# The opening of the last mixture-of-experts stage: weights' rests, cleared rows and the first gathered tiles in another order

## The reference, cut to what matters

```
x: (4, 750, 192) after the stages before; 3000 tokens, D=192, F=768, E=8 experts
n      = layernorm(h)
logits = n @ Ws + bs                       # (tokens, 8)
probs  = softmax(logits);  route = argmax(probs);  prob_max = max(probs)
hid    = gelu(n @ W1[route] + b1[route])   # 192 -> 768
y      = hid @ W2[route] + b2[route]       # 768 -> 192
out    = h + prob_max * y                  # each token goes through one expert
```

## Time and profile before

| | us |
|---|---|
| median of 3 runs (1774.12 to 1779.3) | 1778.48 |
| profiled execution, device time | 1779.27 |
| its span in the trace | 1777.5 |
| last stage: first DVE instruction | 1547.54 |
| list of rows `take` written | 1598.11 |
| first product of the first gathered tile | 1614.67 |
| second gathered tile's turn of the loop begins | 1619.93 |

### The profile page before, as it was taken

One profiled execution on the slowest core, in us unless ns is written; L12 is line 12 of the kernel. 1 busy time (PEld: TensorE's weight loads), 2 busy tenths in 40 slices (PEclk: granted clock), 3 DMA queues, 4 the chain that ended last, 5 costly groups with the idle time before them and its releaser, 6 DMA issues. The chain is left out here.

```text
span 1777.5 us, 32284 instructions
## 1 busy us (share of the span) xinstructions
PE 1545.6 (87%) x10815; PEld 1432.0 (81%) x10816; DVE 1198.3 (67%) x2259; ACT 990.7 (56%) x1818; POOL 343.4 (19%) x507
## 2 busy tenths in 40 slices
PE   4873899945999999899999899899999999646997
PEld 4762899944899899898899899799999889526996
DVE  3878555547785786785787686687777587485553
ACT  6433222224777578577577678577668657262221
POOL 4130566650100110110010010010010000103443
PEclk6886899976998999999899999999999899757999
DMA  8203111145101101100110110110110100191121
GB/s 257 68 23 95 45 56 57 58 118 141 43 11 37 43 11 37 45 11 18 29 43 10 30 44 19 28 43 19 29 43 19 28 8 19 45 311 46 59 61 30
DMA packets 61940, 94.86 MB, mean 53 GB/s; under 512 B 15645, under 2 KB 46512, under 8 KB 61423
## 3 DMA queue, kind: packets, MB, share of 16 engines
q1 hardware_dynamic: 52606, 72.92, 13.9%
q0 software_dynamic: 9200, 20.21, 3.9%
HBM read 72.58 MB, written 21.06 MB: 53 GB/s over the span
## 5 line engine op out<-in xcount | busy, mean ns | idle before, releaser
L2690 DVE TENSOR_TENSOR a_Plo<-a_PT,a_Phi 125x756 fp32r<-125x756 f32 x288 | 281.9, 979 | 72.5 <-ACT a_PT L2415 71.5
L2415 ACT ACTIVATE a_Phi<-a_S 125x756 fp32r<-125x756 f32 x288 | 231.2, 803 | 152.0 <-PE a_O L2209 128.4
L2580 DVE TENSOR_REDUCE a_nmx<-a_M 125x1 f32<-125x752 f32 x248 | 232.7, 938 | 102.9 <-PE a_M L2084 101.9
L1904 POOL TENSOR_TENSOR a_qlo<-a_work,a_qhi 127x750 fp32r<-127x750 f32 x48 | 79.2, 1659 | 1012.6 <-PE a_S L2190 510.9
L2415 ACT ACTIVATE a_PT<-a_S 125x756 f32<-125x756 f32 x288 | 230.3, 800 | 0.0
L1129 PE MATMUL m_psG<-m_w,m_xT 128*128 x788 | 167.3, 351 | 5.1 <-issue 2.3
L2190 PE MATMUL a_S<-a_qhi,a_khi 128*125 128x378 f32 x576 | 153.5, 348 | 10.0 <-DVE a_nmx L2580 6.8
L2202 PE MATMUL a_O<-a_Phi,a_vhi 125*128 125x378 f32 x576 | 150.3, 342 | 1.4 <-issue 1.1
L2209 PE MATMUL a_O<-a_Plo,a_vhi 125*128 125x378 f32 x576 | 147.5, 337 | 0.4 <-DVE a_Plo L2690 0.2
L2190 PE MATMUL a_S<-a_qhi,a_klo 128*125 128x378 f32 x576 | 147.6, 338 | 0.0
L2190 PE MATMUL a_S<-a_qlo,a_khi 128*125 128x378 f32 x576 | 147.0, 336 | 0.0
(11 more groups left out here) (431 smaller groups left out, 3017.1 us busy)
## 6 DMA issues: line engine op xcount, KB each, us to landing
a_qhi<-a_rdens SPq DMA_DIRECT2D x48, 187.5 KB, 3.3
m_w<-in_m_w SPq DMA_DIRECT2D x16, 384.0 KB, 7.2
a_wkv<-a_w4k SPq DMA_DIRECT2D x8, 768.0 KB, 4.9
a_wq<-a_w4q SPq DMA_DIRECT2D x8, 768.0 KB, 6.3
a_wkv<-a_w4v SPq DMA_DIRECT2D x8, 768.0 KB, 5.9
m_w<-in_m_w SPq DMA_DIRECT2D x8, 576.0 KB
m_X<-m_xn SPq DMA_DIRECT2D x8, 504.0 KB
m_w<-in_m_w SPq DMA_DIRECT2D x16, 192.0 KB, 7.5
```

What stands on the lines that cost most here:

```text
L1904: pool.tensor_tensor(qlo[0:ONE, u % HG % QLO, :], work[0:ONE, u % HG, 0:L], qhi[0:ONE, u % HG, :].bitcast(F32), ALU.subtract).then_inc(sg[ ...
L2415: last = nc.scalar.activation(to[:, wd % 2, :].rearrange("p (a l) -> p a l", a=2), psS[wd % 2][0:P, :, 0:HP], ACT.Exp, scale=SCALE)
L2580: v.tensor_reduce(nmx[:, u % 2, c:c + 1], bank[0:P, :, 0:376], AX.XY, ALU.max, negate=True).then_inc(sg["max_ready"], 1)
L2690: v.tensor_tensor(Plo[:, wd % 2, :], PT[:, wd % 2, :], Phi[:, wd % 2, :].bitcast(F32), ALU.subtract).then_inc(sg["exp_rest"], 1)
```

## The change

- `BLO` becomes 65, next to `BHI`. The product with `xB` runs over rows 0 to 65, all of which are written by rest or bias. The eight memsets (L998) go, and with them SP's and PE's waits for them; PE waits for the ones in `xB` through a new semaphore `s_xo`. POOL's four clearing transfers follow `xB` at once.
- The subtraction of a rest is written as `scalar_tensor_tensor` (times 1.0, minus) in place of `tensor_tensor`.
- ACT rounds expert 3 behind the last logits, ahead of the exponentials; DVE makes its rest behind `msk`.
- Behind `take` DVE's queue reads: rests 4, 5, 6, `rest_of_tokens(0, 0)`, rest 7, `rest_of_tokens(0, 1)`, and only then the parts of the probability and `tileP`.
- PE turns the first two gathered tiles without waiting for weights; those waits stand behind the turns, ahead of the first product. That holds for the first mixture too, where nothing else changes.

```
-BHI, BLO = 64, 96
+BHI, BLO = 64, 65
...
-                sp.wait_ge(s_z, 3)
                 sp.wait_ge(s_wb, 18)
...
-                pool.memset(xB[64:128].bitcast(F32), 1.0)
-            if not cfg.gated:
-                for e in range(NE):
-                    last = pool.memset(w1[64:128, e, 3, :].bitcast(F32), 0.0)
-                last.then_inc(s_z, 1)
-                pool.wait_ge(s_z, 3)
+                pool.memset(xB[64:128].bitcast(F32), 1.0).then_inc(s_xo, 1)
+                pool.wait_ge(s_xo, 1)
...
-            pe.wait_ge(s_eid, 1)
-            pe.wait_ge(s_w, 16 * (NE + (0 if cfg.gated else 3)))
-            if not cfg.gated:
-                pe.wait_ge(s_wl, NE)
-                pe.wait_ge(s_z, 3)
             for j in range(2):
                 pe.wait_ge(s_in[j], 16)
                 if j:
                     pe.wait_ge(s_xc, 1)
                 to_columns(j)
             pe.wait_ge(s_xc, 2)
+            pe.wait_ge(s_eid, 1)
+            pe.wait_ge(s_w, 16 * (NE + (0 if cfg.gated else 3)))
+            if not cfg.gated:
+                pe.wait_ge(s_wl, NE)
+                pe.wait_ge(s_xo, 1)
...
             logits_out(NT // GROUP - 1)
+            if not cfg.gated:
+                round_weights(soon)
             act.wait_ge(s_ls, 1)
...
-                for e in range(soon, NE):
+                for e in range(soon + 1, NE):
                     round_weights(e)
...
-                v.tensor_tensor(w1[:, e, 1, :], w1[:, e, 1, :].bitcast(F32), w1[:, e, 0, :].bitcast(F32), ALU.subtract)
+                v.scalar_tensor_tensor(w1[:, e, 1, :], w1[:, e, 1, :].bitcast(F32), 1.0, w1[:, e, 0, :].bitcast(F32),
+                                       ALU.mult, ALU.subtract)
...
                 v.tensor_copy(msk[:], oh[:, 0]).then_inc(s_m, 1)
+                rest_of_weights(3)
...
-                for e in range(3, NE):
+                for e in range(4, NE):
+                    if e == NE - 1:
+                        rest_of_tokens(0, 0)
                     rest_of_weights(e)
+                rest_of_tokens(0, 1)
...
-            rest_of_tokens(0, 0)
-            rest_of_tokens(0, 1)
+            if cfg.gated:
+                for j in range(2):
+                    rest_of_tokens(0, j)
```

More of the change, by code:

```diff
@@ L918, in moe @@
         s_w1 = [] if cfg.gated else [sem(f"w1_{e}") for e in range(NE)]
-        s_wb, s_wh, s_wl = (None if cfg.gated else sem(k) for k in ("wb", "wh", "wl"))
+        s_wb, s_wh, s_wl, s_xo = (None if cfg.gated else sem(k) for k in ("wb", "wh", "wl", "xo"))
         s_xh = sem("xh")
@@ L1308, in rest_of_weights, with rest_of_tokens @@
                 dve.wait_ge(s_wh, e + 1)
-                v.tensor_tensor(w1[:, e, 1, :], w1[:, e, 1, :].bitcast(F32), w1[:, e, 0, :].bitcast(F32), ALU.subtract)
-                v.tensor_tensor(w1[0:64, e, 3, :], w1[0:64, e, 3, :].bitcast(F32), w1[0:64, e, 2, :].bitcast(F32),
-                                ALU.subtract).then_inc(s_wl, 1)
+                v.scalar_tensor_tensor(w1[:, e, 1, :], w1[:, e, 1, :].bitcast(F32), 1.0, w1[:, e, 0, :].bitcast(F32),
+                                       ALU.mult, ALU.subtract)
+                v.scalar_tensor_tensor(w1[0:64, e, 3, :], w1[0:64, e, 3, :].bitcast(F32), 1.0,
+                                       w1[0:64, e, 2, :].bitcast(F32), ALU.mult, ALU.subtract).then_inc(s_wl, 1)
+            def rest_of_tokens(i, j):
+                dve.wait_ge(s_xh, RING * i + (j + 1))
+                v.tensor_tensor(xT[:, j % 2, 1, :], psX[:, 0:SLOT], xT[:, j % 2, 0, :].bitcast(F32), ALU.subtract)
+                v.tensor_tensor(xT[64:128, j % 2, 2, :], psX[0:64, SLOT:2 * SLOT],
+                                xT[0:64, j % 2, 2, :].bitcast(F32), ALU.subtract).then_inc(s_xc, 1)
+                if not cfg.gated:
+                    v.tensor_copy(hres[:, j % RING, :], xg[:, j % RING, E:2 * E]).then_inc(s_hr, 1)
             def normalise(t):
@@ L1501, in _ @@
             v.sem_inc(s_y, 1)
-            def rest_of_tokens(i, j):
-                dve.wait_ge(s_xh, RING * i + (j + 1))
-                v.tensor_tensor(xT[:, j % 2, 1, :], psX[:, 0:SLOT], xT[:, j % 2, 0, :].bitcast(F32), ALU.subtract)
-                v.tensor_tensor(xT[64:128, j % 2, 2, :], psX[0:64, SLOT:2 * SLOT],
-                                xT[0:64, j % 2, 2, :].bitcast(F32), ALU.subtract).then_inc(s_xc, 1)
-                if not cfg.gated:
-                    v.tensor_copy(hres[:, j % RING, :], xg[:, j % RING, E:2 * E]).then_inc(s_hr, 1)
             def gated_hidden(i, j):
```

## The result

The changed kernel takes 1765.95 us (median of 8 executions), the kernel before in the same comparison 1777.53 (8 executions): ratio 0.9941, 95% interval 0.9923 to 0.9959. One of the eight had a granted clock of 0.563 where the others had 0.926 to 0.935 and took 2825.08 us; the ratio leaves it out, and the median of the other seven is 1765.15. A second comparison, with 12 and 17 executions, gave 1768.51 and 1776.13, ratio 0.9952 [0.9934, 0.9970]. The change gains 0.5 to 0.6%, some 9 us. The predicted 1770.5 against 1778.48 is a ratio of 0.9955.

What follows compares the result with a forecast made beforehand. DVE was taken to bound the stretch before the last stage's loop, working 13 us without a gap, and PE the loop behind its first turns. -2.4 + 0.3 - 6.4 + 0.5 = -8.0 us gave 1770.5 us; 8-in-10 range 1767 to 1774.5.

Steps and rivals of the forecast that it cites:

- front: Start of the last stage: without the memsets DVE's first six normalised tiles run faster, last logits 2.4 us earlier.
- expert 3's rounding ahead of the exponentials: On ACT behind the last logits copy: one rounding of 2.44 us delays the exponentials, costing 0.3 us.
- queue behind the list: DVE's new order behind the list of rows: the first product of a gathered tile comes 6.4 us earlier.
- PE's wait for `tileP`: Ahead of the probabilities' products: PE finishes the first products before `tileP` is ready, a new wait costing 0.5 us.
- PE's clock: Around the first products: the clock's rise may move by a microsecond or two either way, half counting: +-1; no chance given.
- turns of the loop: Loop over gathered tiles in the last stage: turns were said to last as long as before.
- The middle of the range: 2.4 us for the front, between 1.9 and 2.9, since which clock PE gets there could not be read.
- the hole of 1.74 us: DVE's wait for PE's counts, said to hold expert 3's rests of 1.74 us at no cost, 0.1 at most.
- The wait for the first gathered tile: On DVE behind rests 4, 5, 6: 0.96 us of new idle time until gathered tile 0's rest can start.
- The form: DVE's rests as `scalar_tensor_tensor` in place of `tensor_tensor`: no difference in time expected.
- Neither rival on it: Rests in the new form: slower by 0.78 us each, 1781.0, chance 0.04; or POOL freed for gathers, 1769.6, chance 0.12.
- The rule of the Trainium skill: For DVE's rests: the new form with two sources that aren't bf16 runs at half throughput, 0.78 us more each.

Runs made afterwards that it cites:

- x3: Changed kernel with expert 3 rounded behind the exponentials and its rests made behind the list again; one profiled execution took 1767.57 us.
- x8: Changed kernel with the probability's sum and quotient ahead of gathered tile 0's rest, PE's register load and expert 3's first rounding copy earlier; median 1766.96 us, ratio 0.9938.
- x1: Changed kernel with the eight memsets of the third weight rows and the waits for them put back; one profiled execution took 1779.79 us.
- x2: Changed kernel with the rests written as `tensor_tensor` again; one profiled execution took 1766.19 us.
- x7: Changed kernel with PE loading the first expert's register ahead of its waits for tile 1's rest and the weights; one profiled execution took 1765.36 us.
- x11: Changed kernel with thirty transposes of the identity added on PE in each of the two mixtures, run again; median 1758.02 us, ratio 0.9891.
- x12: Changed kernel with thirty transposes of the identity added on PE in the last mixture alone; median 1768.39 us, ratio 0.9952.
- x5: Changed kernel with DVE doing the probability's sum, quotient and parts first behind the list, ahead of the rests; one profiled execution took 1766.12 us.
- x10: Changed kernel with thirty transposes of the identity added on PE in each of the two mixtures, first run; one profiled execution took 1750.82 us.
- x6: Changed kernel with the probability's sum and quotient put into DVE's 0.98 us wait ahead of gathered tile 0's rest; one profiled execution took 1777.52 us.

## Why the prediction was right

The milestones give each term of the sum.

| term | predicted | measured | by |
|---|---|---|---|
| front | -2.4 (-1.9 to -2.9) | -2.2 | A -1.95 less the next row |
| expert 3's rounding ahead of the exponentials | +0.3 | +0.3 | x3 and x8: A 48.3 without, 48.6 with |
| queue behind the list | -6.4 | -6.27 | B 16.56 to 10.29 |
| PE's wait for `tileP` | +0.5 | +0.3 | PE's row at 1609.91 |
| PE's clock | 0 (+-1) | -0.7 | C -0.36 less the row above |
| turns of the loop | 0 | -0.3 | last 157.56 to 157.28, all of it in the second turn's own length (4.92 to 4.62) |
| sum | -8.0 | -8.86 | A, B, C and last |

**The front.** That the memsets slowed DVE's normalised tiles was right (x1), and so was the size. The tiles take 1.92, not the 1.83 of the second batch. The middle of the range was a choice between two clocks of PE, and PE had 1.2 GHz at the last groups again (1.06 us for 16 products, as in the earlier trace rows). For that case the working said 1.9 us, and it was 2.2, so that the forecast of 2.4 was so near is in part luck.

**Expert 3.** The price of 0.3 was right to a tenth, the hole of 1.74 us held both rests, and the gain went mostly into waiting: x3 shows 0.3 us net, which the sum does not state apart.

**The queue behind the list.** The wait for the first gathered tile was worked out from the first mixture's gather, to 0.96; it is 0.98. The first product was said to come near 1606.2 and stands at 1606.08. The step of the argument that carries it, that tile 1's way round PE, ACT and DVE hides behind expert 7's rests, is seen in the row at 1604.59, which has no wait. Its second gather was issued in 1.37 us, not in the 2.24 that the working took over from before; that had no effect, since rest 7 hid it.

**The form.** Neither rival on it came: not slower, since a rest takes 944 ns in the changed kernel against 943 before; nor does it free POOL (x2). The price at 768 columns, which no row of before showed, is that of 192 columns: no difference. The rule of the Trainium skill that the prediction weighs against this does not hold here at either size, for float32.

**What was mis-sized.** PE's clock I left at +-1 without a sign. It rose 3.3 us behind the first product, before it was 5.9 us (the prediction reads 5.5, from a row whose mean of 0.88 puts the rise 0.4 us behind its start). That made up for more than the wait of 0.3: C became shorter by 0.36 where I had it longer by 0.5, and the second turn itself shorter by 0.3. Both together are the whole -1.0 of the stated +-1. "Twice as long" was too much: 1.06 against 0.64 us for 16 products, 1.89 against 1.07 for the probabilities' 24. x7 shows how loosely this hangs on the program: a first product 0.56 us earlier, and the clock came too late for the probabilities. The expected time of 1770.5 was 4.5 above the first median, 2.0 above the second; 0.9 of that is the sum, and the rest is the scatter between executions, of which the three of before said no more than that they lie 5 us apart. So the time itself came out this near partly by luck; the milestones are what bears the mechanism out.

## What to carry to other kernels

When a queue is reordered, work out from another place of the same trace when the moved step's input really lands: one gather of the first mixture gave the new wait as 0.96 us, and it was 0.98. Judge an edit by milestones within its own stage, since those repeated to 0.1 us where whole executions lay 12 us apart. And when executions scatter, look for small transfers that an engine waits for and for what lies across them: here moving the blocks of program code off a round trip through memory gained 10 us, as much as the whole reordering, and most of it at PE's clock.

## What the runs showed of the hardware

- A fetch of program code (16 KB, 0.9 to 1.4 us) holds up small transfers beside it: from the issue of the read-back of the row sums to DVE's next instruction it took 1.5 to 1.75 us without one and 1.9 to 3.2 with one, and DVE went on 1.05 to 1.21 us after the code packet's end. Sixty instructions more on PE, far ahead, moved it out of the way at two to four of the places and made the kernel 10 us faster than the same kernel without them (x11 against x12). In x11 one such packet fell on two other places (waits of 3.25 and 3.18 in place of 1.7 us), so a shift can also lose.
- After a wait of 2.2 us PE worked 13.7 us at 1.2 GHz (x12), after one of 1.0 us 3.4 (x11). At other places falls of 13.7 us and none at all followed waits of 1.6 us.
- Eight memsets of 64x768 on POOL make DVE's `tensor_scalar` over 192 columns take 0.79 in place of 0.31 to 0.32 us each, though both engines write different tiles.
- The issue of a gather on POOL took 1.03 us beside DVE instructions of 0.2 to 0.3 us (x5) and 1.4 to 2.2 beside rests of 0.87 us. The form of the rest makes no difference.
- Twenty transposes raised PE's clock to 2.4 GHz, and it was back at 1.2 within the 3.5 us wait behind them (x10).

Left open: whether x11's shift and x8's order together give both their gains, what stretches every fourth turn in x6 and x8, what sets when PE's clock rises (3.0 to 7.7 us behind the first product in these kernels), and what PE's moved waits are worth alone.
